# One buffer per later projection, unit-ordered direct transfers, and ScalarE's attention units without a loop

## What is computed

```
q = x @ Wq;  k = x @ Wk;  v = x @ Wv          # 16 heads of 16; 4 groups for k and v
att = q . k / 4 + slope * (j - i) + causal;  att = softmax(att)
x = layernorm(x + (att @ v) @ Wo)
routed = expert[argmax(x @ router.T)] on x * sigmoid(top logit)
x = layernorm(x + shared(x) + routed)
```

## Time and profile before

| | us |
|---|---|
| median of 3 runs | 568.68 |
| lowest, highest | 566.39, 571.71 |
| profiled execution | 574.12 |
| its span in the trace | 572.4 |
| TensorE busy | 521.7 (91% of the span) |
| VectorE busy | 299.7 (52%) |
| ScalarE busy | 231.4 (40%) |
| GpSimd busy | 172.3 (30%) |

### The profile page before, as it was taken

One profiled execution on the slowest core, in us unless ns is written; L12 is line 12 of the kernel. 1 busy time (PEld: TensorE's weight loads), 2 busy tenths in 40 slices (PEclk: granted clock), 3 DMA queues, 4 the chain that ended last, 5 costly groups with the idle time before them and its releaser, 6 DMA issues.

```text
span 572.4 us, 7851 instructions
## 1 busy us (share of the span) xinstructions
PE 521.7 (91%) x2538; PEld 259.4 (45%) x2538; DVE 299.7 (52%) x624; ACT 231.4 (40%) x465; POOL 172.3 (30%) x240
## 2 busy tenths in 40 slices
PE   5868899999799999998987899989999999999991
PEld 2433333333233333331245754655666565656661
DVE  1759888888678888882045734212212233333332
ACT  3523376767476767677820121001012222232320
POOL 4413111413031313121201106860003545454543
PEclk9979899999989999999977889998999999999997
DMA  7759501927152727210224600221112222222220
GB/s 219 144 146 313 130 23 49 251 75 207 50 135 78 177 82 181 77 38 21 73 81 149 205 0 1 92 93 38 55 52 60 69 61 74 65 74 65 59 53 27
DMA packets 39465, 54.97 MB, mean 96 GB/s; under 512 B 5887, under 2 KB 27971, under 8 KB 39316
## 3 DMA queue, kind: packets, MB, share of 16 engines
q1 hardware_dynamic: 29792, 30.96, 20.7%
q0 software_dynamic: 5952, 19.56, 11.0%
q10 hardware_dynamic: 3680, 3.94, 2.1%
HBM read 34.76 MB, written 17.52 MB: 91 GB/s over the span
## 4 chain that ended last, share of the span: by engine, by line
PE 80%; DVE 6%; ACT 4%; SPq 3%; issue 2%; DMA 1%; another core or an unknown queue 1%; POOL 1%; POOLq 0%; ACTq 0%; DVEq 0%
PE ps L734 14%; PE ps L554 12%; PE ps L529 11%; PE ps L654 10%; PE ps L543 9%; PE ps L753 7%; PE ps L665 5%; DVE mx L895 4%; PE ps L626 3%; PE ps L499 2%; PE ps L531 2%; PE ps L745 2%; ACT probs L820 2%; PE ps L643 1%; SPq L376 1%
## 5 line engine op out<-in xcount | busy, mean ns | idle before, releaser
L895 DVE TENSOR_REDUCE mx<-ps 128x1 f32<-128x512 f32 (+4 forms) x312 | 184.1, 643 | 39.2 <-PE ps L531 22.8
L820 ACT ACTIVATE probs<-ps 128x512 f32<-128x512 f32 x288 | 153.0, 605 | 74.8 <-PE ps L543 70.1
L529 PE MATMUL ps<-qk_or_dn 127*128 127x512 bf16 (+3 forms) x384 | 119.8, 339 | 4.6 <-DVE mx L895 3.5
L543 PE MATMUL ps<-qk_or_dn 127*128 127x512 bf16 x288 | 101.4, 382 | 6.2 <-ACT probs L820 5.7
L1156 POOL TENSOR_SCALAR_AFFINE_SELECT probs<-probs 128x512 f32<-128x512 f32 x64 | 40.6, 634 | 177.8 <-ACT probs L820 177.8
L734 PE MATMUL ps<-wgu,tmp 128*128 x184 | 82.9, 593 | 0.1
L554 PE MATMUL ps<-probs,Vs 128*32 128x512 f32 x576 | 77.1, 608 | 0.7 <-ACT probs L820 0.7
L529 PEld LDWEIGHTS ps<-qk_or_dn 127*128 127x128 bf16 x384 | 37.8, 99 | 78.7 <-DVE mx L895 65.0
L531 PE MATMUL ps<-cb 128*128 128x128 bf16 x256 | 51.8, 227 | 0.0
L1200 POOL DMA_INDIRECT rows<-acc,tok x23 | 22.5, 979 | 91.5 <-DMA acc<-x_all 46.7
L1084 DVE TENSOR_TENSOR tmp<-tmp,ps 128x512 f32<-128x512 f32 x23 | 15.8, 688 | 65.1 <-PE ps L734 65.1
(11 more groups left out here) (117 smaller groups left out, 467.7 us busy)
## 6 DMA issues: line engine op xcount, KB each, us to landing
wgu<-in_gu POOLq DMA_DIRECT2D x8, 1024.0 KB, 6.4
qk_or_dn<-qparts SPq DMA_DIRECT2D x36, 128.0 KB
yT<-yU SPq DMA_DIRECT2D x16, 256.0 KB, 2.4
qk_or_dn<-in_dn SPq DMA_DIRECT2D x8, 512.0 KB, 8.0
tmp<-xs SPq DMA_DIRECT2D x23, 128.5 KB
qparts<-tmp SPq DMA_DIRECT2D x6, 384.0 KB, 4.3
tmp<-yT SPq DMA_DIRECT2D x34, 64.0 KB
xs<-rows POOLq DMA_DIRECT2D x1, 2056.0 KB, 12.8
```

The costliest lines, as they stand in the source:

```text
L529: mm = pe.matmul(o, q, K6[k][0:KROWS, k0:k0 + w], start=True, stop=not masked)
L543: pe.matmul(o, K6[k][0:KROWS, kb * P:(kb + 1) * P], Q6[k][0:KROWS, :, qi * P:(qi + 1) * P], start=True, stop=True).then_inc(s_st, 1)
L820: act.activation(probs[:, 4 * (s % 3) + p, :], ps[:, 4 + (4 * s + p) % SB, :], ACT.Exp, scale=SCALE).then_inc(s_exp, 1)
L895: dve.tensor_reduce(o, ps[:, a_bank(u, t), 0:nh * w].rearrange("p (h w) -> p h w", h=nh), AX.X, ALU.max).then_inc(s_amax, 1)
```

## The change

Three things. The part buffers of the eight later jobs are no longer three in turn in `tmp` but eight of their own in `wgu`, behind `wide`; the wait of ScalarE for a landed store is gone, and the three semaphores of the stores become one. The direct transfers are ordered by unit: unit 0 for c = 0 and c = 1, the constant rows of unit 1, then unit 1 for c = 0 and c = 1. ScalarE's loop over six units is written out as eight units in a row; SyncE's loop stays.

```diff
--- before.py
+++ after.py
@@ -91,7 +91,6 @@
     (2, 1), (3, 1)]
 NJ = len(JOBS)
 DIRECT = 4
-NP = 3
 FIRST_A, LATE_AT, ACT_CASTS = 4, 9, 6
 Q_AT, K_AT = (0, (3, 5), 4), (2, (0, 5), 1)
 A_TILES = row_max_tiles()
@@ -171,10 +170,11 @@
         cb = sb("cb", [P, CB_N], BF16)
 
         tmp = sb("tmp", [P, 4096 + 2 * (C + 1)])
-        t16 = tmp[:, 0:3 * 3 * CH // 2].bitcast(BF16)
-        parts0 = [t16[:, r * 3 * CH:(r + 1) * 3 * CH].rearrange("p (a t) -> p a t", a=3) for r in range(3)]
         wide16 = wgu[:, 0:DIRECT * 3 * CH].bitcast(BF16)
         wide = [wide16[:, n * 6 * CH:(n + 1) * 6 * CH].rearrange("p (s t) -> p s t", s=6) for n in range(DIRECT)]
+        t16 = wgu[:, DIRECT * 3 * CH:DIRECT * 3 * CH + (NJ - DIRECT) * 3 * CH // 2].bitcast(BF16)
+        parts0 = {n: t16[:, (n - DIRECT) * 3 * CH:(n - DIRECT + 1) * 3 * CH].rearrange("p (a t) -> p a t", a=3)
+                  for n in range(DIRECT, NJ)}
         vT = tmp[NG * D:P, 3840:3840 + CH]
         rest0 = [tmp[:, 2304 + r * CH:2304 + (r + 1) * CH] for r in range(3)]
         yTc = [tmp[:, i * 1024:(i + 1) * 1024].rearrange("p (k t) -> p k t", k=KC) for i in range(3)]
@@ -239,7 +239,7 @@
         s_xT = [sem(f"s_xT{i}") for i in range(NCH)]
         s_prj, s_ph, s_pr, s_pm, s_pl, s_vT, s_vps, s_vev = (
             sem(n) for n in ("s_prj", "s_ph", "s_pr", "s_pm", "s_pl", "s_vT", "s_vps", "s_vev"))
-        s_pw = [sem(f"s_pw{i}") for i in range(NP)]
+        s_pw = sem("s_pw")
         s_copies, s_kw = sem("s_copies"), sem("s_kw")
         s_dir = [[sem(f"s_dir{i}{c}") for c in range(2)] for i in range(2)]
         s_one, s_seen = [sem(f"s_one{i}") for i in range(STEP)], sem("s_seen")
@@ -407,11 +407,11 @@
             load_rows(0)
             load_unit_head(0, 0)
 
-            for c in range(2):
-                for i in range(2):
+            for i in range(2):
+                for c in range(2):
                     direct_q(i, c)
                     direct_k(i, c)
-                if c == 0:
+                if i == 0:
                     load_rows(1)
                     load_unit_head(1, 1)
             for c in range(2):
@@ -426,11 +426,10 @@
                 else:
                     r, m, dst = b * NG * D, NG * D, kparts_d
                 sp.dma_start(dst[:, r:r + m, col:col + CH].rearrange("a r t -> r a t"),
-                             parts0[n % NP][0:m, :, :]).then_inc(s_pw[n % NP], 16)
+                             parts0[n][0:m, :, :]).then_inc(s_pw, 16)
             max_rows(0, 0)
             sp.wait_ge(s_kw, 64)
-            for i in range(NP):
-                sp.wait_ge(s_pw[i], 16 * sum(n % NP == i for n in range(DIRECT, NJ)))
+            sp.wait_ge(s_pw, 16 * (NJ - DIRECT))
             with sp.Fori(0, LOOPS, 1) as it:
                 for k in range(STEP):
                     step(it * STEP + k, k)
@@ -796,9 +795,7 @@
                                    wide[n][0:m, high:high + 1, :].broadcast_to([m, 2, CH]), ACT.Copy
                                    ).then_inc(s_copies, 1)
                 else:
-                    if n >= DIRECT + NP:
-                        act.wait_ge(s_pw[n % NP], 16 * ((n - DIRECT) // NP))
-                    act.activation(parts0[n % NP][0:m, 0, :], ps[0:m, 4 + n % 4, :], ACT.Copy).then_inc(s_ph, 1)
+                    act.activation(parts0[n][0:m, 0, :], ps[0:m, 4 + n % 4, :], ACT.Copy).then_inc(s_ph, 1)
                 i = 2 * (n - LATE_AT)
                 for dst, src, done in later_loads[i:i + 2] if i >= 0 else []:
                     act.dma_start(dst, src.rearrange("(k p) n -> p k n", p=P)).then_inc(done, 16)
@@ -810,7 +807,7 @@
                     put_values(JOBS[n - 1][0])
                 if n >= ACT_CASTS:
                     act.wait_ge(s_pr, n + 1)
-                    act.activation(parts0[n % NP][0:m, 1, :], rest0[n % 3][0:m, :], ACT.Copy).then_inc(s_pm, 1)
+                    act.activation(parts0[n][0:m, 1, :], rest0[n % 3][0:m, :], ACT.Copy).then_inc(s_pm, 1)
 
             def weights(u, s):
                 for p in range(4):
@@ -834,10 +831,7 @@
                 act.activation(yU[:, 1, :], ps[:, 3, :], ACT.Copy).then_inc(s_yev, 1)
 
             weights(0, 0)
-            with act.Fori(0, LOOPS, 1) as it:
-                for k in range(STEP):
-                    step(it * STEP + k)
-            for u in range(LOOPS * STEP, NU):
+            for u in range(NU):
                 step(u, last=u == NU - 1)
 
             for c in range(NCH):
@@ -899,7 +893,7 @@
                 m = P if JOBS[n][1] < 2 else NG * D
                 rest = rest0[n % 3][0:m, :]
                 high, middle, _ = Q_AT if JOBS[n][1] < 2 else K_AT
-                h = wide[n][0:m, high, :] if n < DIRECT else parts0[n % NP][0:m, 0, :]
+                h = wide[n][0:m, high, :] if n < DIRECT else parts0[n][0:m, 0, :]
                 dve.wait_ge(s_ph, n + 1)
                 if n >= 3:
                     dve.wait_ge(s_pl, n - 2)
@@ -911,7 +905,7 @@
                     dve.tensor_copy(md, rest.rearrange("p (o t) -> p o t", o=1).broadcast_to([m, 2, CH])
                                     ).then_inc(s_pm, 1)
                 elif n < ACT_CASTS:
-                    dve.tensor_copy(parts0[n % NP][0:m, 1, :], rest).then_inc(s_pm, 1)
+                    dve.tensor_copy(parts0[n][0:m, 1, :], rest).then_inc(s_pm, 1)
                 if n >= FIRST_A:
                     for t in first_tiles(n):
                         reduce_tile(0, t)
@@ -1124,7 +1118,7 @@
                 if n < DIRECT:
                     lo, md = wide[n][0:m, low, :], wide[n][0:m, middle[0], :]
                 else:
-                    lo, md = parts0[n % NP][0:m, 2, :], parts0[n % NP][0:m, 1, :]
+                    lo, md = parts0[n][0:m, 2, :], parts0[n][0:m, 1, :]
                 pool.tensor_tensor(lo, rest0[n % 3][0:m, :], md, ALU.subtract).then_inc(s_pl, 1)
             pool.wait_ge(s_vinit, 2)
             pool.wait_ge(s_vev, NCH)
```

## The result

The changed kernel took 562.76 us (median of 4, from 560.35 to 564.5) against 568.75 before (566.39 to 571.71), a ratio of 0.990 with the 95% interval 0.986 to 0.993. Measured again, the same code came to 0.989 (0.985 to 0.993). So it gains about 6 us where the forecast said 10.6. The time lies inside the wide range of 554.5 to 564, which had been drawn to reach Rivals A and B, and outside the forecast's own range of 555 to 561. Two single executions of later runs, one of the changed kernel (1047.20 us) and one of the new order alone (1048.25 us), took nearly twice the time and are left out of the ratios; why is open. The profiled execution took 564.5 us, its span 562.8.

What follows compares the result with a forecast made beforehand. TensorE held 80% of the chain, so gains were sought where it waits: 5.2 + 0 + 5.4 = 10.6 us off 568.68, forecast 558.0 us; own range 555 to 561, 8-in-10 range 554.5 to 564.

Steps and rivals of the forecast that it cites:

- Rival A: First (projection) stage: gives the time back; if only 1 of 5.2 us is kept, 562.3 us; chance 0.10.
- Rival B: ScalarE at unit 3: the gap stays, from a fetch or something else; 563.5 us; chance 0.08.
- Part one: First stage, part buffers: without ScalarE's wait for a stored part, lot 9 starts 5.2 us earlier (bounds 4.1 to 5.7).
- That copy started 2.66 us after the job's first copy: First stage, job 9: the second `vT` copy, behind ScalarE's loads, was assumed to keep this delay from the old trace.
- The bound of 4.1: First stage, part buffers: the least gain expected, in us, if TensorE's clock does not recover.
- Part two: SyncE's queue, reordered direct transfers: everything behind moves back 1.5 us at no cost; gain 0, between 0 and 0.5 us.
- the delay costs nothing: SyncE's queue: the 1.5 us delay is harmless, as unit 1's operands are read at about 52, covered by 15 us.
- unit 0's early half: Direct transfers: unit 0's second half comes about 4 us earlier, but its reader in lot 6 gains nothing.
- Part three: ScalarE's attention units: writing out the loop removes the 4.47 us gap at unit 3, gaining 5.4 us (4.5 to 5.5).
- Inside the units nothing changes: Attention units: the same 36 exponentials and two copies, so each unit still takes 28.39 us.
- both move forward with the jobs, so they meet the same neighbours: First stage: the argument that VectorE's work and ScalarE's load issuing shift with the jobs, so no time is given back.
- Rival C: ScalarE's units: straight code stalls on fetches too, at 5.46 us each; three stalls give 574.5 us; chance 0.04.

Runs made afterwards that it cites:

- the waiting mask and the old order: Changed kernel with GpSimd's eighth-group mask waiting for VectorE's last split subtraction, and direct transfers in the old order: ratio 0.979 of before.
- once more: The changed kernel profiled and timed again, unedited: ratio 0.989 of before (0.985 to 0.993).
- the loads behind the maxima: Changed kernel, GpSimd's eighth-group mask waiting for VectorE's last split subtraction, six late loads issued from SyncE after unit 0's row maxima: ratio 0.977 of before.

## Why the prediction was right or wrong

**The number.** The range held, but by its reach to Rivals A and B, and the 10.6 was too much by 4.6. Two steps failed, one in the first stage and one in the units, and the range holding is in part luck.

**Part one.** Right in mechanism and in size: lots 7 and 8 came within 0.35 us of the forecast, the granted clock was 1.00 from 34 to 46, and with the old order the whole term measured 5.3 (eight buffers alone). The step that failed is the one where the loss behind the loads was taken over from the trace of before: "That copy started 2.66 us after the job's first copy". With the old order this still held (2.65 with eight buffers alone, 2.11 with the waiting mask and the old order). In the changed kernel it came to 5.22 (43.38 against 38.16), and 3.81 once more. The figure of before was read at loads issued at 43, when the stores of the first four jobs were through. In the changed kernel the loads are issued at 37.6, and stores of four jobs begin at 34.8. The bound of 4.1 for this part did not hold either: counted from lot 6 the term came to 1.4, 2.2, 4.4 and 5.2 in the four executions with the new order.

**Part two.** I gave it 0 to 0.5 gained. It loses. The 1.5 us by which SyncE's queue moves back were worked out rightly and show in the new order alone; in the changed kernel's four executions the first store came 4.5 to 5.2 after lot 6 against 2.6 to 2.9 with the old order, 1.6 to 2.6 later. But "the delay costs nothing" was wrong: I asked who waits for the stores, and not what the stores collide with. On the traces the first exponential comes 30.30 to 34.06 after lot 6 with the new order and 29.89 to 30.43 with the old; the means of four and three executions, 32.2 and 30.2, are 2.0 apart. The timed ratios, 0.984 and 0.989 to 0.990 in separate measurements, agree with that and don't prove it. The gain from unit 0's early half is nil, as said.

**Part three.** The gap, its cause at the jump and its price on the path were right; the gap went. The step that failed is "Inside the units nothing changes". In straight code the mask comes 0.07 us earlier against VectorE's reduction (114.20 - 112.56 = 1.64 before, 113.59 - 112.02 = 1.57 after), and that was enough to turn round a race that stood at 0.05 us. ScalarE's timeline shows where: before, it stood 0.16 us between the first and the second exponential of that group (the second starts at 113.54), and after, three run from 112.24 without such a gap. It costs 6 x 0.46 = 2.76 of the 5.46. The 0.05 us stood in the trace of before and I did not look for it. Unit 6, which I had taken as the witness since it was written out already, could not have shown it: TensorE has fewer tiles there, the mask starts 1.49 us behind the subtraction (259.35 against 257.86), and the subtraction takes 0.19 in both kernels.

**The sum as it came out.** With 5.3 for the buffers, 5.46 - 2.76 = 2.7 for the loop and 2.0 for the collision it is 6.0 us, and 6.0 was measured. That it fits so well is chance in part: the collision came to between -0.1 and 4.2 in single pairs of executions and the jump to between 3.36 and 6.99, so each term is known to a microsecond or two.

**The rivals.** Rival A, time given back in the first stage, is what happened in part, though for a cause that I had argued against: "both move forward with the jobs, so they meet the same neighbours". The stores didn't move with them. Rival B fell. Rival C fell in its own form, no fetch held ScalarE in the units of any run with straight code, but a cost on every unit of straight code was there, by another road.

## What to carry to other kernels

When one transfer is moved earlier, look for what it now meets in the DMA engines and not only for who waits for it: loads and stores that used to miss each other collided, and a small urgent transfer behind 3.8 MB on its own queue took 7.6 us where the median was 1.8. When an engine is made faster by a few hundredths of a microsecond, look for pairs on VectorE and GpSimd that start close together, and ask which order is the costly one; the wait that fixed the cheap order cost nothing that the pitch shows. A unit with less work in it is no witness for the others.

## What the runs showed of the hardware

A VectorE subtraction of two SBUF operands of 128x32 takes 0.19 us alone and 0.65 when a GpSimd mask of 0.64 has started 0.02 before it; started 0.05 ahead of the mask it keeps its 0.19, and the mask its 0.64. The lost time stands in the profile as a longer instruction and in no list of waits. The Trainium skill describes such a lock ("SBUF — State Buffer", SBUF: two separate sides: VectorE with two SBUF inputs and GpSimd share one pair of ports, whoever starts first holds it for the whole instruction); by that rule, the trace agrees for the mask ahead, with the end of the subtraction at 114.26 and of the mask at 114.23. For the subtraction ahead it does not show: the mask should have been held until 114.34 and so have taken some 0.78, and no mask in the kernel before took more than 0.654. That ScalarE is slower in a hardware loop than in straight code shows only as the 0.07 and 0.16 us above; what in it takes the time was not looked into. The jump back held ScalarE for 2.67, 2.74, 4.47 and 4.93 us in four kernels and cost the path 3.36, 5.96, 5.46 and 6.99.

Outside the change, VectorE waits in the expert stage, at an addition to `x_all`, for something that the profile only calls remote (another core or an unknown queue), and by very different amounts. The list of waits, before and with the loads behind the maxima:

```profile
DVE x_all L1072 <- remote: 4.5, 1, 4.5
```

```profile
DVE x_all L1064 <- remote: 9.6, 2, 7.8
```

In both profiles of the changed kernel there is none, and in five of the others it is 3.8. The profiled executions before and after differ by 9.6 us in their spans, of which 3.7 lie ahead of the end of the last exponential (288.8 against 285.1) and 5.9 behind it, in code that is the same; this wait is 4.5 of these. It is why spans of single executions are not compared here. Its cause stays open.
